# Rows scattered without the last layer norm, which the experts fold into their own norm, gate and epsilon

## The chip, the cores and the metric

The kernel runs on one core of one Trainium2 chip. The metric is device time in microseconds (us) of one execution, lower is better. The engines are PE (matrix products), DVE (VectorE), ACT (ScalarE), POOL (GpSimd) and SP (the engine that issues most transfers).

## The reference

Two transformer layers over 2 batches of 2048 tokens with 256 features:

```python
x = _layernorm(x + _L0_attn_ref(x, ...))     # causal attention with ALiBi, 16 heads
x = _layernorm(x + _L0_ffn_ref(x, ...))      # sparse product in frequency space
x = _layernorm(x + _L1_attn_ref(x, ...))     # channel attention, then its own norm, gamma and beta
x = _layernorm(x + _L1_ffn_ref(x, ...))      # routed experts
```

`_layernorm(x)` is `(x - mean) / sqrt(var + 1e-5)`. The last layer routes each token to one of 8 experts:

```python
aff = x @ centroids.T
eid = argmax(aff)
alpha = sigmoid(sum(x * centroids[eid]))
xn = (x - mean(x)) * rsqrt(var(x) + 1e-5)
xln = xn * ln_g[eid] + ln_b[eid]
ffn = relu(xln @ w1[eid] + b1[eid]) @ w2[eid] + b2[eid]
out = x + alpha * ffn
```

The x that enters the experts is the output of the third layer norm. Its mean is zero and its variance is var/(var + eps), so a norm of it can be worked out from the moments of the row before that norm.

## The kernel before

Tokens are handled in 8 tiles (g = 0 to 7) of 512 tokens, each of four 128-token blocks; batch 0 is tiles 0 to 3. The first layer's attention fills the first 920 us and is not touched.

**The back stage.** A planner (`BackPlan`) writes, once, a fixed order of steps for each engine: it takes again and again the step that could start first by its own cost estimates. The order in which PE uses turned tiles is a list written by hand, `TURNS`: O (output product of attention 0), S (spectral product), C (channel product of attention 1), A (affinities with the centroids). Each C tile goes: turn on PE (L1417), copies by ACT (L1782), product on PE (L1444, L1449), squares by ACT (L1811) and one root (L1814), `Scale` on DVE (L2067, L2073), `ShiftBeta` on POOL (L2470), `Combine` on DVE (L2081). The result is the row x before the third layer norm. Each A tile goes: turn (L1417), copies (L1782), `Affinity` (L1468), copy (L1788), turn back (L1476), then on DVE `Best` (L2194 to L2199, which expert), `Choose`, on PE `Count`, on DVE `PlaceRows` (the row's place among its expert's rows), and on POOL `Scatter` (L2484), which sends four blocks of rows to DRAM by indirect transfers.

For each of the 8 tiles the third layer norm is: `Moments` on DVE (4 of L2003, 4 of L2007), `Roots` on ACT (L1761), `Shift` on DVE (L2091, L2094) and `End` on ACT (4 of L1800), which normalises the rows in place. `Best` multiplies the largest affinity by this norm's inverse root (L2195) and stores it beside the row for the gate. `Scatter` waits for `End`.

After `PlaceRows(4)` the step `ChooseSoon` finds the experts of the first three slot tiles. SP then reads three row numbers and, once all products are done, fetches rows for slot tiles 0 to 2. `normalise_rows(0)` stands inside `PlaceRows(7)`, the last route.

**The expert stage.** 39 slot tiles of 128 rows. PE does for each `turn` (L1623), `hide` (L1635, product with w1) and `unhide` (L1647, product with w2). The steady loop of PE is hide(i+1), turn(i+2), unhide(i). That of DVE is turn_own(i+2), which reads the expert's number by `value_load` (L1612) and writes gain and shift (L2323), rectify(i+1) (L2343), normalise(i+3), finish(i), and in every third pass gates for three tiles. That of ACT is rectify, the two roots (L1761) and in every third pass three exponentials (L1871) for the gates. The rows' norm on DVE reads:

```python
take_moments(dve, m, s, n, [row])        # L2003, L2007
invert_roots(dve, m, s, n, 1)            # L2013, waits for ACT's root, L1761
dve.tensor_scalar(m.xn[i % 2], row, m.moments[:, n % NORMS, 0, 0:1], m.rstd[:, n % NORMS, 0:1], ALU.subtract, ALU.mult)
```

Of the kernel before, what the change touches and what calls it, by code (L numbers as in the profile page):

```python
# [14 lines left out]
P = 128  # L15
# [35 lines left out]
SOON = 3  # L51
# [3 lines left out]
NORMS = 4  # L55

# [489 lines left out]
Roots = namedtuple("Roots", "i eps")  # L546
Shift = namedtuple("Shift", "i stage g")
End = namedtuple("End", "i stage g turned")
# [26 lines left out]
Scatter = namedtuple("Scatter", "route normed")  # L575
# [6 lines left out]
def last_with(banks, route, bank):  # L582
# [7 lines left out]
    " C0 C1 C2 C3 A0 A1 C4 A2 C5 A3 C6 C7 A4 A5 A6 A7").split()]  # L590


class BackPlan:
# [7 lines left out]
    def __init__(self):  # L601
# [3 lines left out]
        self.todo = [(stage, g) for stage in "OSCFA" for g in range(TILES)]  # L605
# [164 lines left out]
    def norm_choices(self):  # L770
# [5 lines left out]
        for stage in "OSF":  # L776
            for g in range(TILES):
                if (stage, g) in self.norm_of:
                    continue
                ready = self.at(("second", g) if stage == "F" else ("add", stage, g))  # L780
                if ready is not None:
                    yield max(ready, last), 2, self.moments, (i, stage, g, max(ready, last))
                    break

    def moments(self, i, stage, g, ready):
# [3 lines left out]
        if stage == "F":  # L789
            self.todo.remove((stage, g))  # L790
# [7 lines left out]
    def root(self, i):  # L798
        self.n_rooted += 1
        self.run("act", Roots(i, 0), self.ROOTS, self.done["moments", i], ("roots", i))  # L800
# [12 lines left out]
    def end_choices(self):  # L813
        i = next((i for i in range(self.n_ended, self.n_shifted) if self.norms[i][0] != "O"), None)
        if i is not None:
            stage, g = self.norms[i]
            ready = self.at(("shift", i), *([("turn", self.turn_of.get(("A", g)))] if stage == "F" else []))
            if ready is not None:
                yield ready, 1, self.end, (i, ready)

    def end(self, i, ready):
# [3 lines left out]
        turned = 2 * self.turn_of["A", g] + 2 if stage == "F" else 0  # L825
        self.run("act", End(i, stage, g, turned), self.APPLY, ready, ("end", stage, g), ("end of", i))
# [88 lines left out]
    def route_choices(self, engine):  # L915
        for r, tiles in enumerate(ROUTES):
            for kind, on, step, cost, needs in (
                    ("hot", "dve", Best(r), 1300,
                     [("affinity turned", tiles[-1]), ("gram", tiles[-1] // TPB), ("shift of", "F", tiles[-1])]
# [6 lines left out]
                    ("scatter", "pool", Scatter(r, 0), 1270 * BPT * len(tiles),  # L926
                     [("place", r), ("end", "F", tiles[-1])] + [("scatter", r - 1)] * (r > 0))):
# [3 lines left out]
                if ready is not None:  # L931
                    if kind == "scatter":
                        step = step._replace(normed=self.end_of["F", tiles[-1]])
# [35 lines left out]
class Memory:  # L969


    def __init__(self, nc, ctx, t, out):
# [6 lines left out]
        def carve(at, shape, dt=F32, parts=P):  # L979
# [5 lines left out]
            if len(shape) > 1:  # L985
# [9 lines left out]
        self.eps_col = sb("eps_col", [P, 3])  # L995
# [24 lines left out]
        self.rstd_of = {stage: self.part_max[0][:, i * 2:i * 2 + 2, :, :].rearrange("p a h c -> p (a h c)")  # L1020
                        .rearrange("p (g r) -> p g r", g=TILES) for i, stage in enumerate("OF")}
        pairs = [half.rearrange("p (a r) -> p a r", a=2) for row in (self.neg_max, self.max_rest)
                 for half in (row[:, 0:2 * BPT], row[:, 2 * BPT:])]
        self.squares, self.std_c, self.rstd_c, self.top = pairs
# [125 lines left out]
class Signals:  # L1150


    def __init__(self, nc, ctx):
# [42 lines left out]
        self.rows_chosen = sem("rows_chosen")  # L1196
# [562 lines left out]
def root_moments(act, m, s, i, rows, eps):  # L1759
    act.wait_ge(s.moment, i + 1)  # L1760
    act.activation(m.std[:, i % NORMS, 0:rows], m.moments[:, i % NORMS, 0:rows, 1], ACTF.Sqrt,  # L1761
                   bias=m.eps_col[:, eps:eps + 1]).then_inc(s.rooted, 1)


def rstd_place(m, step):

    return m.rstd[:, step.i % NORMS, :] if step.stage == "S" else m.rstd_of[step.stage][:, step.g, :]


def scalar_back(nc, m, s, plan):  # L1770
    act = nc.scalar
    b0, b1 = FOLD_BANKS
    act.wait_ge(s.vector_set, 4)
    for step in plan.act:
# [15 lines left out]
        elif isinstance(step, Roots):  # L1790
            root_moments(act, m, s, step.i, BPT, step.eps)

        elif isinstance(step, End):
            j = step.i % NORMS
            act.wait_ge(s.norm_shift, plan.end_of[step.stage, step.g])
            if step.turned:
                act.wait_ge(s.turned, step.turned)
# [64 lines left out]
def scalar_experts(nc, m, s, plan):  # L1862
# [25 lines left out]
    root_moments(act, m, s, row_norm[0], 1, 0)  # L1888
    root_moments(act, m, s, row_norm[1], 1, 0)
    scalar_pads(nc, m, s)  # L1890
    gates(range(SOON))
    rectify_own(0)
# [944 lines left out]
```

## Time and profile before

| | |
|---|---|
| median of 3 runs | 1398.23 us (1397.38 to 1404.84) |
| the profiled execution's own time | 1393.97 us |
| span of the profile | 1392.2 us |
| PE busy over the span | 1329.6 us (96%) |
| DVE busy | 1069.0 us (77%) |
| ACT busy | 837.8 us (60%) |
| POOL busy | 263.8 us (19%) |

The span is from the first to the last instruction. The 1.8 us between span and the execution's own time are start and end. Busy shares are means over stages with different limits, so a stage has to be read by itself; the rows below do that for the channel and routing stage (1037 to 1097 us from the span's start) and for the experts (1098 us to the end).

### The profile page before, as it was taken

What the parts mean: (1) busy time and instruction counts of PE and PEld (TensorE: products, weight loads), DVE (VectorE), ACT (ScalarE), POOL (GpSimd) and SP (SyncE); (2) the same over time, 40 slices, a digit from 0 to 9 for tenths busy, and PEclk for the clock granted to TensorE, in tenths of its full rate; (3) what the DMA queues carried; (4) which work ended last, traced back from release to release, by engine and by line L of the source; (5) the groups of instructions that cost most, each with busy time, mean ns of one, the idle gap of its engine ahead of it and who ended that gap; (6) DMA issues with size and microseconds to landing.
All of it is one profiled execution on the core that took longest, in us unless ns stands there. A gap on an engine that the chain in (4) does not pass through costs nothing. (4 is left out here: it accounts for less than half of the span.)

```text
span 1392.2 us, 45529 instructions
## 1 busy us (share of the span) xinstructions
PE 1329.6 (96%) x19104; PEld 801.5 (58%) x19104; DVE 1069.0 (77%) x1991; ACT 837.8 (60%) x1767; POOL 263.8 (19%) x440
## 2 busy tenths in 40 slices
PE   8999999999999999999999999999987699999998
PEld 3544334434444444444444444587766589999997
DVE  2567989989899899899898992476567777766776
ACT  3446668778788688686886886533347333343342
POOL 4332012102111121121021111100126411111111
PEclk9999999999999999999999999999999899999999
DMA  7795401212112212112210000303616565445441
GB/s 228 219 213 133 80 17 37 46 32 50 41 40 46 44 31 48 42 40 48 69 49 4 3 3 2 119 31 117 239 32 212 194 226 181 167 176 186 169 176 71
DMA packets 78230, 134.44 MB, mean 97 GB/s; under 512 B 12370, under 2 KB 64843, under 8 KB 72652
## 3 DMA queue, kind: packets, MB, share of 16 engines
q1 hardware_dynamic: 60556, 109.63, 27.2%
q10 hardware_dynamic: 14064, 13.47, 3.1%
q0 software_dynamic: 3408, 8.43, 1.7%
q8 instruction: 152, 2.49, 0.8%
q14 instruction: 50, 0.41, 0.1%
HBM read 68.01 MB, written 23.11 MB: 65 GB/s over the span
## 5 line engine op out<-in xcount | busy, mean ns | idle before, releaser
L1964 DVE TENSOR_REDUCE part_max<-pair 128x2 f32<-128x1024 f32 (+2 forms) x576 | 641.8, 1158 | 63.0 <-PE pair L1329 32.0
L1748 ACT ACTIVATE big<-pair 128x512 f32<-128x512 f32 (+1 forms) x1120 | 580.2, 610 | 150.7 <-PE pair L1360 142.6
L1360 PE MATMUL pair<-big 128*32 128x512 bf16 (+3 forms) x5120 | 346.5, 349 | 6.7 <-DMA big<-max_t 2.8
L1329 PE MATMUL pair<-big 128*32 128x512 bf16 (+3 forms) x5120 | 340.9, 348 | 11.4 <-DVE part_max L1964 9.4
L1382 PE MATMUL pair<-big 128*17 128x512 f32 (+3 forms) x2560 | 288.2, 529 | 0.9 <-POOL big L2447 0.8
L1329 PEld LDWEIGHTS pair<-big 128*32 128x32 bf16 x5120 | 129.3, 96 | 185.6 <-DVE part_max L1964 94.2
L1360 PEld LDWEIGHTS pair<-big 128*32 128x32 bf16 x5120 | 126.8, 96 | 188.8 <-ACT big L1748 118.8
L1761 ACT ACTIVATE std<-moments,eps_col 128x1 f32<-128x1 f32 (+1 forms) x102 | 30.1, 295 | 235.0 <-DVE moments L2007 235.0
L1635 PE MATMUL pair<-big,tok 128*128 128x128 f32 x1248 | 148.0, 277 | 5.3 <-DVE big L2323 5.1
L1635 PEld LDWEIGHTS pair<-big,tok 128*128 128x128 f32 x1248 | 146.6, 194 | 9.4 <-DVE big L2323 7.7
L2447 POOL TENSOR_SCALAR_AFFINE_SELECT big<-big 128x512 f32<-128x512 f32 x128 | 80.0, 635 | 323.3 <-ACT big L1748 323.3
L1647 PE MATMUL pair<-big 128*128 x624 | 141.0, 379 | 0.0
L1647 PEld LDWEIGHTS pair<-big 128*128 128x128 f32 x624 | 115.6, 190 | 14.1
L1382 PEld LDWEIGHTS pair<-big 128*17 128x17 f32 x2560 | 68.5, 96 | 33.6 <-issue 4.5
L2492 POOL DMA_INDIRECT out<-big x39 | 38.4, 984 | 251.8 <-DVE big L2364 251.8
L1336 PE MATMUL pair<-masks,ident_b 128*32 128x64 bf16 x2048 | 86.1, 193 | 0.0
L1336 PEld LDWEIGHTS pair<-masks,ident_b 128*32 128x32 bf16 x2048 | 53.8, 97 | 28.9 <-issue 25.3
L1268 PE MATMUL pair<-big 128*32 128x512 f32 x512 | 60.0, 613 | 1.1 <-issue 0.8
L2323 DVE TENSOR_SCALAR big<-pair,cent_columns 128x128 f32<-128x128 f32 x78 | 28.4, 406 | 35.9 <-issue 27.7
L1880 ACT ACTIVATE big<-pair,cent_columns 128x128 f32<-128x128 f32 x156 | 44.3, 365 | 18.5 <-issue 11.0
L1933 DVE SCALAR_TENSOR_TENSOR big<-pair,big 128x512 f32<-128x512 f32 x32 | 22.1, 692 | 38.7 <-ACT big L1726 38.7
L2419 POOL TENSOR_TENSOR big<-big 128x512 bf16<-128x512 f32 x32 | 37.0, 1163 | 65.9 <-ACT big L1731 65.9
(213 smaller groups left out, 1209.2 us busy)
## 6 DMA issues: line engine op xcount, KB each, us to landing
tok<-big SPq DMA_DIRECT2D x39, 1024.0 KB, 4.7
big<-in_L_ffn_w SPq DMA_DIRECT2D x16, 1024.0 KB, 14.3
big<-split_dram SPq DMA_DIRECT2D x216, 64.0 KB, 2.9
split_dram<-big ACTq DMA_DIRECT2D x32, 384.0 KB, 4.4
big<-split_dram SPq DMA_DIRECT2D x42, 256.0 KB, 4.3
big<-routed_dram SPq DMA_DIRECT2D x39, 129.0 KB, 2.1
big<-in_c_query_rows SPq DMA_DIRECT2D x8, 512.0 KB, 4.8
big<-in_L_attn_x SPq DMA_DIRECT2D x8, 512.0 KB, 4.5
```

The source lines that it names most:

```text
L1268: mm = pe.matmul(m.bank[b][q:q + STRIPE, :], m.w_qkv0[side][:, c, o:o + STRIPE], m.x_t[step.tile % 2][:, c, :], start=(c == 0), stop=(c == ...
L1329: mm = pe.matmul(bank[q:q + STRIPE, o:o + w], m.q_op[slot][:, step.qt, h, step.r * P + q:step.r * P + q + STRIPE], m.k_op[slot][:, h, step ...
L1336: mm = pe.matmul(bank[q:q + STRIPE, o + w - P + half:o + w - P // 2 + half], m.ident_b[:, q:q + STRIPE], m.masks[:, 1, half:half + P // 2] ...
L1360: mm = pe.matmul(m.bank[step.bank][k:k + STRIPE, n * w:(n + 1) * w], m.k_op[slot][:, h, step.kb * P + k:step.kb * P + k + STRIPE], m.q_op[ ...
L1382: mm = pe.matmul(m.sums[32 * h:32 * h + HD + 1, q0:TILE], m.v_aug[:, b * BPB + kb, g * GH + h, :], m.p_ring[:, place, h, at:at + TILE - q0 ...
L1635: mm = pe.matmul(m.bank[b][:, j * P:(j + 1) * P], w1[:, c, f * P:(f + 1) * P], m.xln_t[i % 2][:, c, :], start=(c == 0), stop=(c == KC - 1))
L1647: mm = pe.matmul(m.bank[b][:, 0:D], m.hidden_t[i % 2][:, f, :], m.w2[:, bass.ds(e, 1), f, :].rearrange("p a n -> p (a n)"), start=(f == 0) ...
L1748: act.activation(m.p_ring[:, step.place, step.heads[0]:step.heads[-1] + 1, step.at:step.at + w], m.bank[step.bank][:, 0:len(step.heads) * ...
L1880: done = act.activation(m.hidden_t[i % 2][:, j, :], m.bank[b][:, j * P:(j + 1) * P], ACTF.Relu, bias=col[:, j, bass.ds(e, 1)])
L1964: dve.tensor_reduce(m.part_max[(step.u * QT + step.qt) % 2][:, step.r, step.heads[0]:step.heads[0] + n, step.c], banks[:, :, 0:w], X, ALU. ...
L2447: pool.affine_select(weights, weights, pattern=[[0, GH], [1, P]], compare_op=ALU.is_ge, fill=zero, base=0, channel_multiplier=-1).then_inc ...
L2492: pool.indirect_dma_start(m.out_rows, bass.IndirectOffsetOnAxis(ap=m.xs[i % ROWS_AHEAD][:, D + 1:D + 2].bitcast(I32), axis=0), m.final[i % ...
```

## The change

The third layer norm is no longer applied in the back stage. The steps `Moments`, `Roots`, `Shift` and `End` of stage F are gone for all 8 tiles. `Scatter` waits for `Combine` in place of `End`. The centroids are stored with the sign turned, so that `Best` takes the least value and writes it straight beside the row (one operation, L2195, goes). The rows that reach the experts are the rows before the norm. For each slot tile DVE works out `row_eps`, ACT takes two roots in place of one (the second for both norms together), DVE inverts the two at once, the gate's exponential takes its scale and bias from columns in place of immediates, the gate is scaled by the first inverse root, and the root of the result takes its epsilon from `row_eps`. The first three gates are made later in the order (on DVE behind `choose_rows`, on ACT behind the first rectify and the third root). In `TURNS` the tile A4 moves ahead of C6 and A5 ahead of C7.

```diff
 TURNS = ...
     "O0 O1 O2 S0 O3 S1 S2 S3 O4 O5 O6 S4 O7 S5 S6 S7"
-    " C0 C1 C2 C3 A0 A1 C4 A2 C5 A3 C6 C7 A4 A5 A6 A7").split()]
+    " C0 C1 C2 C3 A0 A1 C4 A2 C5 A3 A4 C6 A5 C7 A6 A7").split()]
...
-        for stage in "OSF":
+        for stage in "OS":
...
-                    ("scatter", "pool", Scatter(r, 0), 1270 * BPT * len(tiles),
-                     [("place", r), ("end", "F", tiles[-1])] + [("scatter", r - 1)] * (r > 0))):
+                    ("scatter", "pool", Scatter(r), 1270 * BPT * len(tiles),
+                     [("place", r)] + [("scatter", r - 1)] * (r > 0))):
...
+def root_row(act, m, s, i, n):
+
+    k, var = i % ROWS_AHEAD, m.moments[:, n % NORMS, 0, 1:2]
+    act.wait_ge(s.moment, n + 1)
+    act.activation(m.row_std[:, k, 0:1], var, ACTF.Sqrt, bias=m.eps_col[:, 0:1])
+    act.activation(m.row_std[:, k, 1:2], var, ACTF.Sqrt, bias=m.eps_col[:, 2:3], scale=1.0 + EPS).then_inc(s.rooted, 1)
+
+
+def root_result(act, m, s, i, n):
+    act.wait_ge(s.moment, n + 1)
+    act.activation(m.std[:, n % NORMS, 0:1], m.moments[:, n % NORMS, 0, 1:2], ACTF.Sqrt,
+                   bias=m.row_eps[:, i % ROWS_AHEAD, :]).then_inc(s.rooted, 1)
...
-            act.wait_ge(s.rows_in[k], 16 * (i // ROWS_AHEAD + 1))
-            act.activation(m.gate[:, k:k + 1], m.xs[k][:, D:D + 1], ACTF.Exp, scale=-1.0).then_inc(s.gate_exp, 1)
+            act.wait_ge(s.xn_set, i + 1)
+            act.activation(m.gate[:, k:k + 1], m.xs[k][:, D:D + 1], ACTF.Exp, bias=m.eps_col[:, 3:4],
+                           scale=m.row_rstd[:, k, 0:1]).then_inc(s.gate_exp, 1)
...
         elif isinstance(step, Moments):
-            if step.stage == "F":
-                dve.wait_ge(s.combined, step.g + 1)
             take_moments(dve, m, s, step.i, m.norm_rows(step.stage, step.g))
...
-            top = m.top[:, i % 2, :]
+            least = m.tok[:, blocks, D]
...
-            step_done(dve.tensor_reduce(top, affinity, X, ALU.max))
-            dve.tensor_tensor(m.tok[:, blocks, D], top, m.rstd_of["F"][:, tiles[0], :], ALU.mult).then_inc(s.rows_chosen, 1)
-            step_done(dve.tensor_tensor(equal, affinity, wide(top, shape, 2), ALU.is_equal))
+            step_done(dve.tensor_reduce(least, affinity, X, ALU.min))
+            step_done(dve.tensor_tensor(equal, affinity, wide(least, shape, 2), ALU.is_equal))
...
 def normalise_rows(dve, m, s, i, n):
-    row = m.xs[i % ROWS_AHEAD][:, 0:D]
-    dve.wait_ge(s.rows_in[i % ROWS_AHEAD], 16 * (i // ROWS_AHEAD + 1))
+
+    k = i % ROWS_AHEAD
+    row, mean, var = m.xs[k][:, 0:D], m.moments[:, n % NORMS, 0, 0:1], m.moments[:, n % NORMS, 0, 1:2]
+    dve.wait_ge(s.rows_in[k], 16 * (i // ROWS_AHEAD + 1))
     take_moments(dve, m, s, n, [row])
-    invert_roots(dve, m, s, n, 1)
+    dve.wait_ge(s.moment, n + 1)
+    dve.tensor_scalar(m.row_eps[:, k, :], var, EPS, EPS / 4, ALU.add, ALU.mult)
+    dve.wait_ge(s.rooted, n + 1)
+    dve.reciprocal(m.row_rstd[:, k, :], m.row_std[:, k, :]).then_inc(s.norm_inverse, 1)
+    dve.wait_ge(s.norm_inverse, n + 1)
     if i >= 2:
         dve.wait_ge(s.tile_turned, i - 1)
-    dve.tensor_scalar(m.xn[i % 2], row, m.moments[:, n % NORMS, 0, 0:1], m.rstd[:, n % NORMS, 0:1], ALU.subtract,
-                      ALU.mult).then_inc(s.xn_set, 1)
+    dve.tensor_scalar(m.xn[i % 2], row, mean, m.row_rstd[:, k, 1:2], ALU.subtract, ALU.mult).then_inc(s.xn_set, 1)
...
             dve.wait_ge(s.gate_exp, i + 1)
-            dve.tensor_scalar(g, g, 1.0, 2.0, ALU.add, ALU.mult).then_inc(s.gate_sum, 1)
+            dve.tensor_scalar(g, g, 2.0, m.row_rstd[:, k, 0:1], ALU.add, ALU.mult).then_inc(s.gate_sum, 1)
...
-    gates(range(SOON))
     rectify(0)
     normalise(2)
     turn_own(2)
     rectify(1)
     choose_rows(dve, m, s, step_done)
+    gates(range(SOON))
     finish(0)
...
-            pool.wait_ge(s.rows_chosen, step.route + 1)
-            pool.wait_ge(s.normed, step.normed)
+            pool.wait_ge(s.combined, tiles[-1] + 1)
```

## Rows read from the trace of the kernel before

**Rows 1.** Busy time by stretch: stretch, length, each engine (instructions), clock, DMA.

```profile
1150.00:1200.00 50.00, 50.00 (x348) 47.21 (x347) 34.68 (x124) 20.33 (x56) 6.88 (x7) 1.00 0.49 179
```

**Rows 2.** Timeline of one pass of the expert loop: start, length, engine, idle before.

```profile
1206.14 0.73 DVE L2323 TENSOR_SCALAR big<-pair,cent_columns 128x128 f32<-128x128 f32 x2 [0.73 <-issue]
...
1208.28 0.18 DVE L2007 BATCH_NORM_AGGREGATE moments<-stats 128x2 f32<-128x6 f32 x1
1208.49 0.29 ACT L1761 ACTIVATE std<-moments,eps_col 128x1 f32<-128x1 f32 x1 [1.57 <-DVE moments L2007]
1208.82 0.16 DVE L2013 RECIPROCAL rstd<-std 128x1 f32<-128x1 f32 x1 [0.36 <-ACT std L1761]
...
1213.13 0.73 DVE L2323 TENSOR_SCALAR big<-pair,cent_columns 128x128 f32<-128x128 f32 x2 [1.13 <-issue]
```

**Rows 3.** Waits from 1155 to 1376 us: total, times, longest.

```profile
DVE big L2323 <- issue: 25.4, 29, 1.3
...
DVE recip_l L2331 <- ACT recip_l L1871: 8.3, 10, 0.9
...
DVE big L2323 <- PE pair L1623: 1.6, 2, 1.1
```

**Rows 4.** Line L1612, the load of an expert's number: shortest/median/longest ns.

```profile
L1612 DVEq TENSOR_LOAD <-tile_expert x39: 302/562/998, 1091.2 to 1374.1; - x39
```

**Rows 5.** Groups by line and shape from 1100 us: count, busy us, mean ns.

```profile
L2323 DVE TENSOR_SCALAR big<-pair,cent_columns 128x128 f32<-128x128 f32 x76 | 27.7, 407 | 35.9 <-issue 27.7 <-PE pair L1623 8.2
...
L1761 ACT ACTIVATE std<-moments,eps_col 128x1 f32<-128x1 f32 x76 | 22.4, 295 | 164.5 <-DVE moments L2007 164.5
```

**Rows 6.** The same view, further down: the gates' exponentials.

```profile
L1871 ACT ACTIVATE recip_l<-big 128x1 f32<-128x1 f32 x39 | 5.0, 192 | 0.1
```

**Rows 7.** Groups by line and shape from 1000 to 1095 us.

```profile
L2484 POOL DMA_INDIRECT routed_dram<-tok,position x28 | 28.2, 1008 | 17.6 <-DVE position L2228 10.4 <-issue 7.2
...
L1800 ACT ACTIVATE tok<-tok,shift,part_max 128x256 f32<-128x256 f32 x32 | 16.6, 596 | 0.5 <-DVE shift L2094 0.5
...
L1811 ACT ACTIVATE big<-pair 128x256 f32<-128x256 f32 x28 | 10.4, 377 | 8.6 <-PE pair L1449 8.6
```

**Rows 8.** Timeline: a root on ACT and the instruction right behind it.

```profile
1066.15 0.30 ACT L1814 ACTIVATE neg_max<-neg_max,eps_col 128x4 f32<-128x4 f32 x1
...
1066.35 1.06 ACT L1782 ACTIVATE big<-pair 128x512 f32<-128x512 f32 x2
```

**Rows 9.** Timeline of channel tiles 5 to 7 and the affinity tiles behind.

```profile
1048.55 2.07 ACT L1800 ACTIVATE tok<-tok,shift,part_max 128x256 f32<-128x256 f32 x4
...
1050.68 1.07 ACT L1782 ACTIVATE big<-pair 128x512 f32<-128x512 f32 x2
...
1051.80 0.39 PE L1444 MATMUL pair<-acc_t,part_max 128*128 128x512 bf16 x1 [0.64 <-ACT big L1782]
...
1059.24 1.23 DVE L2081 TENSOR_TENSOR tok<-tok,big 128x1024 f32<-128x1024 f32 x1
...
1061.18 0.39 PE L1444 MATMUL pair<-acc_t,part_max 128*128 128x512 bf16 x1 [0.64 <-ACT big L1782]
...
1067.97 0.38 PE L1444 MATMUL pair<-acc_t,part_max 128*128 128x512 bf16 x1
...
1075.58 1.09 PE L1417 MATMUL pair<-ident,tok 128*128 128x128 f32 x8
...
1078.67 1.09 PE L1417 MATMUL pair<-ident,tok 128*128 128x128 f32 x8
```

**Rows 10.** Timeline of the last route and the first expert tile.

```profile
1082.22 0.14 PEld L1476 LDWEIGHTS pair<-ident,masks 128*128 128x128 f32 x1 [0.66 <-ACT masks L1788]
...
1088.43 0.19 DVE L2194 TENSOR_REDUCE max_rest<-pair 128x4 f32<-128x32 f32 x1
...
1092.30 0.43 DVE L2003 BATCH_NORM_STATS2 stats<-big 128x6 f32<-128x256 f32 x1 [1.14 <-DMA big<-routed_dram]
...
1097.85 5.53 PE L1635 MATMUL pair<-big,tok 128*128 128x128 f32 x32 [1.90 <-DVE big L2323]
```

More of the change, by code:

```diff
@@ L545 @@
 Moments = namedtuple("Moments", "i stage g")
-Roots = namedtuple("Roots", "i eps")
+Roots = namedtuple("Roots", "i")
 Shift = namedtuple("Shift", "i stage g")
-End = namedtuple("End", "i stage g turned")
+End = namedtuple("End", "i stage g")
 ShiftBeta = namedtuple("ShiftBeta", "g m")
@@ L574 @@
 PlaceRows = namedtuple("PlaceRows", "route")
-Scatter = namedtuple("Scatter", "route normed")
+Scatter = namedtuple("Scatter", "route")
 Busy = namedtuple("Busy", "count")
@@ L604, in __init__ @@
         self.done = {"loaded": 9000}
-        self.todo = [(stage, g) for stage in "OSCFA" for g in range(TILES)]
+        self.todo = [(stage, g) for stage in "OSCA" for g in range(TILES)]
         self.turns, self.turns_used, self.uses = [], 0, 0
@@ L779, in norm_choices @@
                     continue
-                ready = self.at(("second", g) if stage == "F" else ("add", stage, g))
+                ready = self.at(("add", stage, g))
                 if ready is not None:
@@ L799, in root @@
         self.n_rooted += 1
-        self.run("act", Roots(i, 0), self.ROOTS, self.done["moments", i], ("roots", i))
+        self.run("act", Roots(i), self.ROOTS, self.done["moments", i], ("roots", i))
     def shift_choices(self):
@@ L816, in end_choices @@
             stage, g = self.norms[i]
-            ready = self.at(("shift", i), *([("turn", self.turn_of.get(("A", g)))] if stage == "F" else []))
-            if ready is not None:
-                yield ready, 1, self.end, (i, ready)
+            ready = self.done["shift", i]
+            yield ready, 1, self.end, (i, ready)
     def end(self, i, ready):
@@ L824, in end @@
         self.end_of[stage, g] = len(self.end_of) + 1
-        turned = 2 * self.turn_of["A", g] + 2 if stage == "F" else 0
-        self.run("act", End(i, stage, g, turned), self.APPLY, ready, ("end", stage, g), ("end of", i))
+        self.run("act", End(i, stage, g), self.APPLY, ready, ("end", stage, g), ("end of", i))
     def squares_choices(self):
@@ L918, in route_choices @@
                     ("hot", "dve", Best(r), 1300,
-                     [("affinity turned", tiles[-1]), ("gram", tiles[-1] // TPB), ("shift of", "F", tiles[-1])]
+                     [("affinity turned", tiles[-1]), ("gram", tiles[-1] // TPB)]
                      + [("hot", r - 1)] * (r > 0)
@@ L931, in route_choices @@
                 if ready is not None:
-                    if kind == "scatter":
-                        step = step._replace(normed=self.end_of["F", tiles[-1]])
                     yield ready, 0, self.run, (engine, step, cost, ready, (kind, r))
@@ L1790, in scalar_back @@
         elif isinstance(step, Roots):
-            root_moments(act, m, s, step.i, BPT, step.eps)
+            root_moments(act, m, s, step.i)
         elif isinstance(step, End):
```

69 lines of the change are left out of this document (34 added, 35 removed).

## The prediction

> **What bounds the kernel now.** I read the busy time by stretch first, and it misleads: from 1150 to 1200 us PE is busy for all 50.00 us and DVE for 34.68 [rows 1]. That looks like a PE bound with 30% of DVE to spare. The view of waits says otherwise. Between 1155 and 1376 us DVE's first step of a pass waited for PE twice, for 1.6 us in all, while its idle time is "issue", 25.4 us in 29 passes, and the gates' wait for ACT, 8.3 us in 10 [rows 3]. So DVE walks its loop without ever being held by PE for long: its idle time lies inside its own chain. One pass took 6.99 us from L2323 to L2323 [rows 2]. In it the chain is moments, ACT's root, inverse: 0.36 us of DVE idle while ACT works 0.29 us [rows 2]. The "issue" time is the load of the expert's number ahead of L2323, 0.30 to 1.00 us with a median of 0.56 [rows 4]. The reader is to see that PE and DVE run level, and that whatever lengthens DVE's serial chain lengthens the kernel, though DVE's share is 70%.
>
> The other stretch that counts is serial as well. From the channel product of C4 to the first hide, each C tile with an A tile takes 9.38 us (product of C5 at 1051.80, of C6 at 1061.18), the C tile without one 6.79 (C7 at 1067.97), an A tile alone 3.09 (turns at 1075.58 and 1078.67) [rows 9]. The last route was turned back at 1082.22, but its `Best` began at 1088.43, behind `ChooseSoon`, the last `Moments` and two routes on DVE; the first rows' norm began at 1092.30 and hide(0) at 1097.85 [rows 10].
>
> **The change, part by part. Removed from the back stage.** 32 of L1800 (16.6 us of ACT) [rows 7], 32 statistics on DVE, 8 roots, 8 `Shift`. Most of it lay beside PE's work. What sat on the path is ACT's order: `End` ran from 1048.55 to 1050.62, so the copy of the affinity and the copies of C5 at 1050.68 stood behind it and the product waited 0.64 us for them [rows 9]. Without `End` the copies could begin when the first half of the turn is there; I take 0.7 us for each of C5 and C6 and 0.8 for C4, bounds 0.3 and 1.2 each. C7 gains nothing new (next term). Sum: 2.2 us earlier. Of the fold of batch 1 I expect nothing: its waits are for PE and DVE steps that stay.
>
> **Moved: A4 ahead of C6, A5 ahead of C7.** A4 adds an A tile, 3.09 less the 0.4 that `End` cost there, 2.7. C6 to C7 grows from 6.79 to 9.38 less 0.7, 8.7: 1.9. One more `Count` on PE: 0.4. So C7's product starts 2.7 + 1.9 + 0.4 - 2.2 = 2.8 us later, at 1070.8. In return only A6 and A7 lie behind it. From the start of a C product to the end of its `Combine` is 1059.24 + 1.23 - 1051.80 = 8.7 us [rows 9]; from the turn of A7 to its turn back 1082.22 + 0.33 - 1078.67 = 3.9, without `End` 3.5 [rows 9, 10]. So `Best(7)` could start at 1070.8 + 8.7 + 3.5 + 0.3 for hand-overs = 1083.3 in place of 1088.43, since `ChooseSoon` (its route 4 is done before C6) and routes 4 to 6 are behind DVE by then. From `Best(7)` to the first rows' norm was 1092.30 - 1088.43 = 3.87 us [rows 10], with one `PlaceRows` in it that can now come earlier; I take 3.3, so that norm begins at 1086.6. Head start: 5.7 us, bounds 2 and 10. SP's fetch of the first rows hangs on `ChooseSoon` and C7's product, both past by 1075: hidden, with 10 us to spare. The gates moved on DVE lie ahead of finish(0), whose product is there already; about 0.3 us of them shows at tile 4, whose hide waits for DVE.
>
> **Added to every slot tile.** (a) The second root. A root of one column with a pointer for its bias is 295 ns [rows 5]. A root began at 1066.15 and lasted 0.30, the next instruction began at 1066.35 [rows 8]: a pitch of 0.20. DVE waits for the second, so its idle 0.36 becomes 0.56: 0.20 us. Lower bound 0.10 (the two overlap more), upper 0.30 (not at all). (b) `row_eps` on DVE lies inside that wait: nothing; it needs about one hand-over (0.04) and one small operation, well under 0.36 us; with no cover, 0.2. (c) An inverse of two columns for one: nothing. (d) The exponentials get two pointers for two numbers. Without pointers one takes 192 ns [rows 6]. ACT with two pointers on 256 columns is 596 ns, without 377 [rows 7]: 0.22 for two; one pointer is 295 against 192. The gates' sum on DVE waits 0.83 us on average for the first [rows 3], so 0.20 more, and the following two come slower, 0.05: 0.25 us for each group of three, bounds 0 and 0.5. The gates' sum itself has a pointer for a number: at most the same 0.1, in the upper bound. No engine waits behind ACT for this otherwise.
>
> 34 norms of rows lie in the loop behind hide(4) (slot tiles 5 to 38) and 12 groups of gates: 34 x 0.20 + 12 x 0.25 = 6.8 + 3.0 = 9.8 us, bounds 3.4 (0.10 and 0) and 16. Ahead of it the norms of rows 0 and 1 delay hide(0) by 0.4 us and the one of row 4 delays hide(4) by 0.2; with the gates' 0.3 that is 0.9.
>
> The Trainium skill, ScalarE: Activation LUTs, section What ACT_TABLE_LOAD costs, says that each pointer operand adds about 93 ns to an ACTIVATE and that back-to-back ones overlap by about 93 ns. The traced 295 against 192 ns agrees [rows 5, 6]. An estimate by that page: the second root costs 280 - 93 = 187 ns, the first exponential 186 ns more, and the ones behind it come at 279 ns; the sum would be 6.4 + 3.4. No row shows an exponential with pointers.
>
> **Sum.** -5.7 + 0.9 + 9.8 = +5.0 us on the profiled execution's 1393.97, of which 1392.2 are span: 1399.0. The median of the runs shown is 4.3 us above that execution, so the median comes to 1403.
>
> **Rivals.** (1) Not slower: ACT overlaps the pair of roots (0.10) and the exponentials cost nothing. Then 3.4 + 0.9 - 5.7 = -1.4, and with a head start of 10 us, -5.7: a median of 1392 to 1397. For it: a row with two exponentials back to back would be shorter than their sum. Against it: the pitch of 0.20 behind a root [rows 8]. It decides if DVE's chain grows by less than 0.13 us a tile. (2) POOL becomes the wait. A scatter is 4 x 1.26 = 5.0 us of POOL (1008 ns and 0.26 idle each) [rows 7] and cannot be broken off. If POOL takes up scatter 4 or 5 just ahead of `ShiftBeta(7)`, `Combine(7)` comes up to 4.7 us late and A7, the last route, with it. For it: scatters now wait for less and crowd ahead of C7. Against it: `ShiftBeta` has about 1.3 us to spare, and before one scatter lay there too. Then +9.7, a median of 1408. (3) DVE has room after all: PE sets the pace and the additions vanish, as the shares of rows 1 suggest. Then about -5, 1393. Against it: two waits for PE in 30 passes [rows 3]. (4) The load of the expert's number, 0.30 to 1.00 us for no reason that I can name [rows 4], falls otherwise with the new phases: 0.1 us on its mean is 3.4 us either way. This is part of the range.
>
> **Chances.** Forecast 0.52, rival 1 0.20, rival 2 0.18, rival 3 0.10. The forecast's own range is -1 to +9 us, by the bounds of 0.20 and of the head start; with a tenth left out on each side over all cases it is -5 to +13: 1393 to 1411. A measurement tells about 0.5%, 7 us. Faster than that takes rival 1 or 3 with the largest head start: 0.08. Slower takes rival 2 or the upper third of the forecast: 0.30. Within 0.5%: 0.62.
>
> **What would show each step.** In the profile after: idle of DVE ahead of the inverse of the rows' norm 0.56 us (0.46 in rival 1); the gates' wait near 1.1 us; mean pass of DVE 0.28 us longer and PE with gaps ahead of hide in most passes, so that PE's busy share in the experts falls; hide(0) near 1092.5 (1097 in rival 2, with `Combine(7)` waiting for POOL); C7's product near 1070.8. The prediction is wrong if PE stays without gaps, if the head start is over 10 us because the planner orders the fold otherwise, or if PE waits on a `Count`.

## The result, and the profile after

The changed kernel takes 1405.3 us against 1397.0, medians of 15 runs each; the ratio is 1.006, with a 95% interval of 1.0046 to 1.0074. It is 0.6% slower: 8.3 us, where +5.0 us on the profiled execution and a median of 1403 were forecast. The profiled execution has a span of 1403.2 us against 1392.2.

The busy time of the same stretch as in [rows 1], in the changed kernel:

```profile
1150.00:1200.00 50.00, 49.52 (x339) 46.27 (x339) 35.57 (x127) 19.88 (x58) 6.88 (x7) 1.00 0.48 175
```

PE has lost half a microsecond of the 50 and DVE has gained 0.9. The waits of DVE from 1155 to 1376 us (total, times, longest), to be held against [rows 3]:

```profile
DVE big L2334 <- issue: 22.5, 29, 1.1
DVE recip_l L2343 <- ACT recip_l L1879: 10.9, 10, 1.1
DVE rstd L2022 <- ACT std L1771: 10.5, 29, 0.4
DVE part_max L2278 <- ACT part_max L1766: 10.4, 29, 0.4
```

The gates' wait is 1.09 us in place of 0.83, and the two waits for PE have gone. One norm of the rows, in the timeline of the changed kernel (start, length, engine, idle before); [rows 2] has the old one:

```profile
1207.50 0.42 DVE L2012 BATCH_NORM_STATS2 stats<-big 128x6 f32<-128x256 f32 x1
1207.95 0.18 DVE L2016 BATCH_NORM_AGGREGATE moments<-stats 128x2 f32<-128x6 f32 x1
1208.16 0.15 DVE L2276 TENSOR_SCALAR part_max<-moments 128x1 f32<-128x1 f32 x1
1208.16 0.29 ACT L1765 ACTIVATE part_max<-moments,eps_col 128x1 f32<-128x1 f32 x1 [1.27 <-DVE moments L2016]
1208.37 0.28 ACT L1766 ACTIVATE part_max<-moments,eps_col 128x1 f32<-128x1 f32 x1
1208.68 0.17 DVE L2278 RECIPROCAL part_max<-part_max 128x2 f32<-128x2 f32 x1 [0.36 <-ACT part_max L1766]
```

The second root begins 0.21 us behind the first. From the end of the moments to the inverse it is 1208.68 - 1208.13 = 0.55 us; before it was 1208.82 - 1208.46 = 0.36 [rows 2]. The idle time is still written as 0.36, because the new small operation L2276 (`row_eps`) fills the rest: whoever reads only the idle column sees no change.

Now the view that the prediction did not use: PE's own timeline, by the starts of its first operation in each pass (L1631, the hide product).

```profile
1198.61 3.73 PE L1631 MATMUL pair<-big,tok 128*128 128x128 f32 x32
1202.18 0.38 PE L1619 MATMUL pair<-ident,big 128*128 128x128 f32 x2
1202.39 3.62 PE L1643 MATMUL pair<-big 128*128 x16
1206.60 3.84 PE L1631 MATMUL pair<-big,tok 128*128 128x128 f32 x32 [0.59 <-DVE big L2334]
...
1213.95 3.73 PE L1631 MATMUL pair<-big,tok 128*128 128x128 f32 x32
```

From start to start it is 7.99 us with the idle 0.59 at its end, and 7.35 for the next. From the eleventh tile on PE's passes in the changed kernel go 7.9, 7.35, 7.24, 8.0, 7.35, 7.24, 8.4, 7.35, 7.24 and so on: one in three is long, the one behind the gates, and the other two are at or near 7.24. PE has a gap ahead of hide in 9 passes of the 30 from 1155 to 1376 us, not in most of them as the prediction's sign said:

```profile
PE pair L1631 <- DVE big L2334: 5.6, 9, 0.9
```

In the kernel before, 25 of the 34 passes behind hide(4) are 7.24 or 7.25 us to the hundredth, as if the engine ran free. It nearly did. The rest of this document divides each profile at PE's first product of tile 0, 4 and 38, called hide(0), hide(4), hide(38); these are worked out from the starts in the timelines. The times are us, and the number load is the mean over the loads behind hide(4):

```
kernel                       hide(0)  to hide(4)  to hide(38)  per pass  DVE's number load  span
before                       1097.85     30.48      248.02      7.295        0.61           1392.2
changed                      1100.63     31.91      254.65      7.490        0.49           1403.2
changed, profiled again      1102.59     31.74      255.38      7.511        0.50           1405.7
old turns                    1105.99     32.99      255.98      7.529        0.49           1410.9
new turns alone, on before   1100.69     30.78      246.88      7.261        0.58           1394.2
one root                     1101.65     31.37      250.37      7.364        0.55           1399.2
numbers in the gates         1099.91     31.71      251.70      7.403        0.52           1399.2
gates late                   1101.34     31.73      251.73      7.404        0.68           1400.6
gates late, on before        1098.60     30.88      246.43      7.248        0.80           1391.8
gates late, one root         1098.59     32.05      248.75      7.316        0.69           1395.2
gates late, early load       1101.92     32.57      248.06      7.296        0.48           1398.4
  the same, on before        1102.50     31.02      246.43      7.248        0.57           1395.8
  the same, one root         1103.50     32.57      248.06      7.296        0.51           1400.0
  the same, and old turns    1098.56     31.56      246.43      7.248        0.51           1392.4
```

The ledger of the changed kernel against the one before, profile against profile: hide(0) 2.8 us later, 1.4 more up to hide(4), 6.6 more in the loop, 0.1 behind it; 11.0 in all. Each row is one execution, and hide(0) is counted from the start of the span. The first channel product C0, which lies ahead of everything that the change touches there, already starts anywhere from 990.4 to 996.7 us in these 14 profiles (991.25 before, 991.44 changed, 994.72 in its second profile, 996.68 with the old turns). So differences of hide(0) between rows are not differences of the kernels; the head start is read further down from C3's product, which follows C0's by 27.7 us in every profile.

### The profile page after: what moved, and what is told of

It is laid out like the page before. It is cut to its first block and busy times, and to the rows that moved or that the text cites. A ratio compares the mean times of both kernels' runs of the same rounds, so it can differ in the third digit from the quotient of the medians.

```text
span 1403.2 us, 45417 instructions
## 1 busy us (share of the span) xinstructions
PE 1329.7 (95%) x19078; PEld 798.4 (57%) x19078; DVE 1062.0 (76%) x1943; ACT 836.4 (60%) x1766; POOL 265.2 (19%) x440
## 5 line engine op out<-in xcount | busy, mean ns | idle before, releaser
L1631 PE MATMUL pair<-big,tok 128*128 128x128 f32 x1248 | 148.9, 278 | 15.9 <-DVE big L2334 15.9
L1631 PEld LDWEIGHTS pair<-big,tok 128*128 128x128 f32 x1248 | 146.3, 194 | 22.2 <-DVE big L2334 20.9
L1771 ACT ACTIVATE std<-moments,part_max 128x1 f32<-128x1 f32 x39 | 11.5, 295 | 95.6 <-DVE moments L2016 95.6
L2334 DVE TENSOR_SCALAR big<-pair,cent_columns 128x128 f32<-128x128 f32 x78 | 28.4, 406 | 37.5 <-issue 25.6
L1765 ACT ACTIVATE part_max<-moments,eps_col 128x1 f32<-128x1 f32 x39 | 11.5, 294 | 72.0 <-DVE moments L2016 64.5
```

Of the source, the lines that this page charges most:

```text
L1631: mm = pe.matmul(m.bank[b][:, j * P:(j + 1) * P], w1[:, c, f * P:(f + 1) * P], m.xln_t[i % 2][:, c, :], start=(c == 0), stop=(c == KC - 1))
```

## The experiments

Ratios are to the kernel before, with 95% intervals.

**The order of turns alone, both ways.** The changed kernel with the old order, and the kernel before with the new one:

```
-    " C0 C1 C2 C3 A0 A1 C4 A2 C5 A3 A4 C6 A5 C7 A6 A7").split()]
+    " C0 C1 C2 C3 A0 A1 C4 A2 C5 A3 C6 C7 A4 A5 A6 A7").split()]
```

> The changed kernel with the old order of turns (C6 and C7 ahead of A4 and A5); the norm stays folded. Theory, that moving A4 and A5 forward is close to neutral (it makes C7 later, and saves routes 4 to 6 ahead of the last): C7's product near 1067, Best(7) between 1086 and 1089, hide(0) within 2 us of the changed kernel's 1100.6, and 1.004 to 1.008 of the kernel before. Rival, that the move is what ate the head start: hide(0) at 1095 or earlier, and 1.002 or less. Rival 2, that the 4.5-us stall ahead of hide(0) in the profile belongs to the new order: it is gone here.

> The kernel before with the new order of turns alone; its last norm stays. Theory: the loop is that of before (mean pass 7.28 us), hide(0) moves by -1 to +3 us, and the ratio to before is 0.999 to 1.003. Rival, that the new order itself costs the 0.6%: 1.004 or more, with hide(0) 5 us or more later.

Measured: 1.0065 (1.0051 to 1.008) and 0.9997 (0.9986 to 1.0007). The move of A4 and A5 is worth nothing in either direction; the 0.6% belongs to the fold. Of the details, `Best(7)` at 1090.0 was outside the expected 1086 to 1089, and hide(0) at 1106.0 was later than expected. But this execution was 5.2 us late at C3's product already; counted from there hide(0) comes at 81.6 us, and at 81.5 in the changed kernel. A stall ahead of hide(0), which rival 2 gave to the new order, is here too: from the first rows' norm to DVE's first L2334 it is 8.2 us, 9.8 in the changed kernel and 4.8 before. So it does not belong to the new order.

**One root.** It leaves out the exact second epsilon: rows and gate share 1/sqrt(var + eps).

```
-    act.activation(m.row_std[:, k, 0:1], var, ACTF.Sqrt, bias=m.eps_col[:, 0:1])
-    act.activation(m.row_std[:, k, 1:2], var, ACTF.Sqrt, bias=m.eps_col[:, 2:3], scale=1.0 + EPS).then_inc(s.rooted, 1)
+    act.activation(m.row_std[:, k, 0:1], var, ACTF.Sqrt, bias=m.eps_col[:, 0:1]).then_inc(s.rooted, 1)
```

> The changed kernel with one root per row norm in place of two (it leaves out the exact second epsilon; rows and gate use the same 1/sqrt(var + eps)). Theory, that DVE's chain is the bound and waits for the second root: 0.20 us less in each of 37 norms, 7.4 us in all, 1.001 of before, mean pass 7.29. Rival, that the lengthening of the pass has another cause (the small DVE operations, or where the expert's number load falls): 2 us or less, 1.004 to 1.006 of before.

**Numbers for pointers in the gates.** It leaves out the fold of the norm into the gate.

```
-            act.activation(m.gate[:, k:k + 1], m.xs[k][:, D:D + 1], ACTF.Exp, bias=m.eps_col[:, 3:4],
-                           scale=m.row_rstd[:, k, 0:1]).then_inc(s.gate_exp, 1)
+            act.activation(m.gate[:, k:k + 1], m.xs[k][:, D:D + 1], ACTF.Exp, scale=1.0).then_inc(s.gate_exp, 1)
...
-            dve.tensor_scalar(g, g, 2.0, m.row_rstd[:, k, 0:1], ALU.add, ALU.mult).then_inc(s.gate_sum, 1)
+            dve.tensor_scalar(g, g, 1.0, 2.0, ALU.add, ALU.mult).then_inc(s.gate_sum, 1)
```

> The changed kernel with numbers in place of pointers in the gates' exponential (bias and scale) and in the gates' sum; it leaves out the fold of the norm into the gate. Theory: the exponentials cost 377 ns against 192 and the sum 0.06 us more, 0.37 us a group; 12 groups and the first one give 4.5 to 5 us back, 1.003 of before, and a gate pass is 0.37 us shorter. Rival, that the gates cost no more than I had predicted (0.25) or nothing: 1.004 to 1.006 of before.

Measured: 1.0019 (1.0008 to 1.0029) with one root, 1.0039 (1.0026 to 1.0052) with numbers. The root gives 4.3 us of the loop back (254.65 to 250.37), where 0.20 in each of 37 norms was expected; the numbers give 3.0, where 4.5 to 5 was. The waits of DVE, first with one root, then with numbers:

```profile
DVE part_max L2277 <- ACT part_max L1765: 5.0, 29, 0.2
```

```profile
DVE recip_l L2342 <- ACT recip_l L1879: 9.0, 10, 0.9
```

The wait for the root falls from 10.4 to 5.0 us in 29 norms, 0.19 each, and the one for the exponentials from 1.09 to 0.90. So both terms of the prediction are where it put them. But both repay less than their 34 x 0.19 = 6.5 and 12 x 0.37 = 4.4, and in both the number load of DVE grew, from 0.49 to 0.55 and 0.52 us, which is 2 and 1 us over 34 passes. One exponential takes 377 ns with its two pointers (L1879, mean of 39) and 192 without.

**The changed kernel once more.**

> The changed kernel as it is, profiled once more, to see what of its profile recurs. Theory: the loop is the same to 0.02 us a pass (7.49) with PE's own pass 7.24 to 7.25; the 4.5-us stall of DVE's first L2334 ahead of hide(0) and the late affinity copies at 1062 and 1087 belong to one execution, and hide(0) lies within 3 us of 1100.6. Rival: they recur at the same places to 0.2 us, and are part of the change.

It took 1407.4 us. The loop recurs (7.511 us a pass) and the stall of 4.5 us ahead of hide(0) does not. The late affinity copies do, against the expectation: the one at 1062.50 starts 1.7 us behind the end of its product in the first profile, and the same one 1.7 us behind in the second (1065.57); the last one is 1.4 and 0.9 us late. It gave a second trace of the back stage, used below.

**Gates late.** DVE's sum and inverse of the gates leave the end of one pass for the place just ahead of `finish` in the next; ACT's exponentials stay. Made on the changed kernel, on the one before, and with one root:

```
             normalise(i + 3)
+        if (i - SOON) % 3 == 0:
+            gates([j for j in range(i, i + 3) if j < SLOT_TILES])
         finish(i)
-        if (i - SOON) % 3 == 2:
-            gates([j for j in range(i + 1, i + 4) if j < SLOT_TILES])
```

> The changed kernel with DVE's part of the gates (sum and inverse) moved from the end of one pass to just ahead of finish in the next; ACT's part stays where it is. Theory, that PE's own pass of 7.245 us is the floor and DVE's chain is over it only for want of 0.25 us a pass: the wait of 1.09 us for the exponentials (12 times, 0.38 us a pass) vanishes, DVE falls under PE, the loop gives 8 us back and no more: passes of PE 7.24 to 7.25 throughout, 1.000 of before. Rival 1, that DVE alone bounds: 13 us back, 0.997. Rival 2, that the wait for ACT only moves: 1.004 or more.

> The kernel before with the same move of DVE's part of the gates. Theory, that its loop is already within 1.1 us of PE's own pass (34 x 7.245 = 246.3 of 247.4 us): 0.999 of before, the gates' wait of 0.83 us gone without a return. Rival, the prediction's reading that DVE's chain bounds the loop and PE only runs level: 12 x 0.83 = 10 us back, 0.993.

> The changed kernel with the late gates and with one root per row norm (it leaves out the exact second epsilon). Theory: PE's pass is the floor, so this is the same as with late gates alone, 0.999 to 1.001 of before, and the two savings do not add. Rival, that they add: a further 6 us, 0.993 to 0.996.

Measured: 1.0041 (1.0027 to 1.0056), 0.9988 (0.9977 to 1.0) and 0.9991 (0.998 to 1.0003). The second came as expected, and its rival of 0.993 lies outside the interval. It decides what bounds the kernel before. PE's timeline in it, and DVE's waits:

```profile
1202.02 3.73 PE L1635 MATMUL pair<-big,tok 128*128 128x128 f32 x32
...
1209.27 3.73 PE L1635 MATMUL pair<-big,tok 128*128 128x128 f32 x32
...
1216.51 3.73 PE L1635 MATMUL pair<-big,tok 128*128 128x128 f32 x32
```

```profile
DVE big L2323 <- PE pair L1623: 32.9, 30, 1.4
DVE rstd L2013 <- ACT std L1761: 21.7, 60, 0.4
...
DVE big L2323 <- issue: 1.1, 1, 1.1
```

Ten microseconds of waiting were taken out of DVE's chain and the loop gained 1.6: PE repeats at 7.25 and 7.24 us, and DVE now waits for it in every one of the 30 passes. So 34 x 7.248 = 246.4 us is PE's floor, and the kernel before stood 1.6 us above it. The prediction's rival 3 was right about that kernel.

On the changed kernel the same edit did less than expected. The gates' wait is gone, but DVE still doesn't fall under PE:

```profile
DVE big L2334 <- issue: 25.2, 29, 1.2
DVE part_max L2278 <- ACT part_max L1766: 16.4, 30, 1.5
...
DVE big L2334 <- PE pair L1619: 1.1, 1, 1.1
```

Part of the wait moved: DVE reaches its next moments while ACT is still behind the exponentials, and waits 16.4 us for roots in place of 10.4. The number load took another part: 0.68 us on average in place of 0.49. Rival 2 of that run was right for these, and my 1.000 was wrong.

The third run met its number and not its theory, that the two savings do not add. They do: the loop falls from 251.73 to 248.75 us, because late gates alone had not brought the changed kernel down to PE's pass.

**The number load moved.** It goes to where DVE waits for ACT anyway. Made with late gates on the changed kernel, on the one before, with one root, and with one root and the old order of turns:

```
         take_moments(dve, m, s, n, [mixed])
+        if SOON <= i and i + 3 < SLOT_TILES:
+            experts[i + 3] = chosen_expert(dve, m, s, i + 3)
         invert_root(dve, m, s, n)
```

> The changed kernel (both roots, exact fold) with the late gates and, besides, DVE's load of the expert's number taken from ahead of L2334 to the place between the moments of the result and the inverse that waits for ACT's root. Theory, that late gates alone left the loop at 7.36 us a pass because the number load grew to 0.69 us (it is slow where the transfer of the next w1 fills the DMA engines) and because roots come later behind ACT's table loads: the load now lies beside a wait of 0.36 us, the pass comes to PE's own 7.245 to 7.27, 3 us less than with late gates alone, 1.001 to 1.002 of before. Rival, that the load only moves its time: the idle ahead of the inverse grows by as much, pass 7.36, 1.004.

> The kernel before with late gates and the early number load. Theory: its loop with late gates alone stood at PE's own 7.24 to 7.25 us in every pass, so nothing more comes of it: 0.998 to 0.999 of before. Rival, that DVE's chain still counts somewhere: 0.996 or less.

> The changed kernel with one root per row norm, late gates and the early number load (it leaves out the exact second epsilon). Theory: the loop is at PE's floor (7.245), so what is left against the kernel before is the back stage alone; that has given no head start, so 0.998 to 0.999, the same as the kernel before with late gates. Rival, the prediction's reading that the fold gives 5.7 us ahead of hide(0) once the loop takes nothing back: 0.994 to 0.995.

> The same kernel (one root, late gates, early number load; it leaves out the exact second epsilon) with the old order of turns. Theory: with the old order ChooseSoon ends late, and SP's first fetch of rows hangs on it, so Best(7) comes 2 us earlier than in the kernel before but the first rows' norm does not; 0.998 to 1.000, within 0.1% of the same kernel with the new order. Rival, that the new order is what loses the head start: 0.995.

Measured: 1.0014 (1.0002 to 1.0025), 0.9999 (0.9988 to 1.001), 1.0001 (0.9987 to 1.0014) and 1.0011 (0.9999 to 1.0023). The first is inside its expected 1.001 to 1.002. The second and third lie 0.1% above what was expected, with the expected values in their intervals; the third excludes its rival of 0.994 to 0.995. The fourth, expected at 0.998 to 1.000 and within 0.1% of the third, is 0.1% above it.

In the first, with both roots and all the pointers, every pass of PE but one is 7.24 or 7.25 us, and from hide(5) on PE's product never waits for DVE. The pass behind hide(4) is 8.98 us, because the hide product in it takes 5.47 us in place of 3.84. The clock granted to PE was 0.50 there (the lower of its two levels, 1.2 for 2.4 GHz), after PE had waited 2.4 us for DVE. The last but two figure is the clock:

```profile
1134.70:1138.10 3.40, 3.40 (x18) 3.40 (x18) 2.02 (x8) 2.01 (x4) 0.31 (x1) 0.50 0.77 277
```

Without these 1.6 us its loop would be 246.4 us, PE's floor. The same drop behind hide(4) is in three other profiles with the fold (old turns; gates late, one root; early load, one root) and in none of the four without it; in the other six with the fold the clock stays at 1.00. DVE's waits in the first run:

```profile
DVE rstd L2022 <- ACT std L1771: 18.4, 29, 1.1
DVE big L2334 <- PE pair L1619: 14.9, 19, 1.1
DVE part_max L2278 <- ACT part_max L1766: 14.9, 31, 0.8
```

The fold's cost in the loop behind hide(5) can therefore be hidden. What comes out with the exact fold is still 0.14% slower than the kernel before, 2 us, and its interval just leaves out 1; with one root it is the kernel before, to about 0.1%. No version here beats it by more than its interval.

## Why the prediction came out as it did

**What bounds the kernel: wrong for the kernel before, right for the changed one.** I set aside PE's 50.00 busy microseconds of 50 [rows 1], because DVE hardly ever waited for PE [rows 3]. The step that failed is "So DVE walks its loop without ever being held by PE for long: its idle time lies inside its own chain". The one pass that it measured, 6.99 us [rows 2], was itself shorter than PE's 7.245, so DVE could run faster than PE. DVE had slack, and its number load ate it unseen. Take the 242 such loads between 1130 and 1390 us in seven profiles (before, changed twice, one root, numbers, gates late on both kernels) by the DMA engines' busy share in the load's first 0.3 us. The 72 with a share under 0.3 took 0.304 us on average and at most 0.315; the 137 with 0.9 or more took 0.805, between 0.30 and 1.00. Over all ten profiles with the load in its old place it is 101 loads at 0.307 (one took 0.51) and 198 at 0.795. Two stretches of the changed kernel, each one load, the last but one figure being the DMA engines' busy share:

```profile
1211.46:1211.76 0.30, 0.30 (x3) 0.28 (x2) 0.30 (x1) 0.10 (x1) 0.00 (x0) 1.00 0.29 82
1217.99:1218.94 0.95, 0.95 (x6) 0.85 (x5) 0.40 (x1) 0.35 (x2) 0.00 (x0) 1.00 0.95 354
```

What fills the DMA engines is the transfer of the next w1 (1024 KB, 30 of them from 1150 to 1376 us), which SP issues when PE has hidden a tile. My reading is that a DVE that runs ahead of PE meets that transfer more often, and that one that is late finds it over. The mean load fits this roughly: 0.80 us where DVE waits for PE in every pass, 0.61 before, 0.49 in the changed kernel, but 0.58 with the new turns alone, whose pass is shorter than before. That the transfer lengthens the load is a coincidence in the records, not shown as a cause; no run here took the transfer away. Without the load, DVE's pass was 7.277 - 0.608 = 6.67 us before; with a load of 0.30 it is 6.97, 0.27 below PE's 7.245. In the changed kernel it is 7.490 - 0.487 = 7.00, and 7.31 with the shortest load: over PE. The change used up a slack that the prediction said was not there. That DVE sets the pace of the changed kernel is shown by the runs that shorten its chain and get the loop back, down to PE's 246.4.

**The added roots: right.** 0.20 us a norm was forecast, 0.19 measured, by the pair of starts, by the interval to the inverse, and by taking it away. The Trainium skill, ScalarE: Activation LUTs, section What ACT_TABLE_LOAD costs, has the figures from which the prediction estimated 187 ns; the traces agree.

**The gates: right in place, too small.** 0.25 us a group was forecast. The exponentials made the wait 0.19 longer as worked out (1.09 for 0.90 with numbers). I kept the gates' sum only in the upper bound: with a pointer it takes 0.20 us in place of 0.14, three times a group. That makes 0.37.

**The sum of the loop.** By these terms 34 x 0.19 + 12 x 0.37 = 10.9 us; the passes without their loads grew by 0.335 x 34 = 11.4. The shorter loads gave back 0.12 x 34 = 4.1, and DVE's loop grew by 7.3 where 9.8 was forecast (6.6 between PE's products). The prediction had this as rival 4, "falls otherwise with the new phases: 0.1 us on its mean is 3.4 us". The size was right and the cause was nameable.

**The head start: wrong.** hide(0) was to come 5.7 us earlier, with bounds of 2 and 10, less 0.4 for two norms. It did not come earlier. In us from the start of C3's product (1018.98 before, 1019.17 changed), worked out from the timelines:

```
                      before  forecast  changed  again  gates late, on before
product of C4          23.45     -       21.77   21.80     21.77
product of C5          32.83     -       31.38   31.15     31.38
product of C7          49.00   51.8      54.51   55.41     47.77
Best(7)                69.46   64.3      68.34   71.68     68.22
first rows' norm       73.32   67.6      70.90   74.17     74.59
hide(0)                78.87   73.5      81.46   80.15     80.34
```

Three steps failed.

First, the 2.2 us for `End`. C4's product did begin 1.5 us earlier from the start of the span, at 1040.94, but that is no work of the change: with `End` still in place, "gates late, on before" has the same 21.77 and 31.38 us. The profile before was the odd one. The product L1570 between C3 and C4 took 5.38 us in it, at a granted clock of 0.59, and 3.69 in the other:

```profile
1029.00:1033.00 4.00, 3.38 (x8) 2.73 (x9) 2.16 (x10) 0.63 (x3) 0.00 (x0) 0.59 0.00 0
```

For C5 the step that failed is "the copies of C5 at 1050.68 stood behind it". They stood behind PE's turn as well, which began 1.39 us ahead of them. Without `End` the copies still begin 1.37 us behind the turn. First before, then changed:

```profile
1049.29 1.09 PE L1417 MATMUL pair<-ident,tok 128*128 128x128 f32 x8
```

```profile
1047.80 1.09 PE L1413 MATMUL pair<-ident,tok 128*128 128x128 f32 x8
...
1049.17 1.32 ACT L1792 ACTIVATE big<-pair 128x512 f32<-128x512 f32 x2 [0.95 <-PE pair L1413]
```

So `End` cost PE's path nothing, and I had counted a gain three times that did not exist once.

Second, C7's product was forecast for 1070.8 and began at 1073.68: C5 to C6 took 13.85 us, not 11.8, and C6 to C7 9.28, not 8.7. Of the 2.0 more between C5 and C6, the late affinity copy at 1062.50 has up to 1.7. In the second profile C6 to C7 is 10.39 us, because C6's two products took 2.97 and 2.33 us in place of 1.89 each, at a granted clock of 0.51 (1068.3 to 1071.7).

Third, "`ChooseSoon` ... and routes 4 to 6 are behind DVE by then". They are, because they moved ahead of C6's `Scale`. From C7's product to `Best(7)` 12.5 us was forecast; it took 13.8 in the first profile, of which the late last copy is 1.4, and 16.3 in the second. The eight profiles with fold and new order have 13.8 and 14.0 in two and 15.9 to 16.5 in six. In the second profile of the changed kernel:

```profile
1073.54 2.60 POOL L2482 TENSOR_TENSOR tok<-tok,big 128x256 f32<-128x256 f32 x4
...
1073.82 2.34 DVE L2231 TENSOR_TENSOR spectral<-acc_t,small 1x8 f32<-1x8 f32 x1 [0.20 <-issue]
...
1074.12 0.30 ACT L1822 ACTIVATE neg_max<-neg_max,eps_col 128x4 f32<-128x4 f32 x1
...
1076.84 0.28 DVE L2240 TENSOR_TENSOR spectral<-spectral,small 1x128 f32<-1x128 f32 x1
...
1079.34 0.15 DVE L2254 TENSOR_TENSOR tile_row<-spectral,small 1x3 int32<-1x3 f32 x1
1079.42 0.16 DVE L2076 RECIPROCAL max_rest<-neg_max 128x4 f32<-128x4 f32 x1
1079.61 1.66 DVE L2082 SCALAR_TENSOR_TENSOR big<-pair,max_rest,big 128x256 f32<-128x256 f32 x4
```

The root of C6 is done at 1074.42 and its inverse begins at 1079.42: five microseconds in which DVE works off route 4, with L2231 held up until 1076.16 (see the last section), and the chain of `ChooseSoon` (L2240 to L2254). In the first profile it is 4.2 us. Behind it come `Combine(6)`, then C7's. The end of the last route in the first profile of the changed kernel:

```profile
1081.59 1.23 DVE L2090 TENSOR_TENSOR tok<-tok,big 128x1024 f32<-128x1024 f32 x1
...
1084.70 0.64 PE L1464 MATMUL pair<-big,cent_columns 128*32 128x128 f32 x16 [0.51 <-ACT big L1792]
...
1086.72 0.28 ACT L1798 ACTIVATE masks<-pair 128x128 f32<-128x128 f32 x1 [2.07 <-PE pair L1464]
...
1087.51 0.19 DVE L2201 TENSOR_REDUCE tok<-pair 128x4 f32<-128x32 f32 x1 [2.37 <-PE pair L1472]
...
1090.08 0.43 DVE L2012 BATCH_NORM_STATS2 stats<-big 128x6 f32<-128x256 f32 x1 [1.03 <-issue]
```

`Best(7)` starts at 1087.51 where 1083.3 was forecast (in the second profile at 1094.12), and the copy L1798 starts 1.4 us after the product that it copies has ended, for no reason that the rows show (ends of products are modelled in the profile). With the old order and the fold `Best(7)` comes 65.6 us behind C3's product, but the first rows' norm only 1097.05 - 1090.01 = 7.0 us later. The stage of the kernel before has 6.4 and 6.6 there in two profiles and 3.9 in the one of [rows 10]. My reading is that the fetch of the first rows, which hangs on `ChooseSoon`, holds the norm there; no run moved that fetch by itself. Either order loses what the other gains, which fits that the two turn experiments show nothing. From `Best(7)` to the norm I had 3.3 us and it was 2.6 (2.5 in the second profile); that step was right. So the norm did come 2.2 us earlier in the first profile, where 5.7 was forecast, and the stall behind it took that away.

What is left of the head start is nothing, to about 1 us. From C3's product to hide(0) the eight profiles with fold and new order take 79.7 to 82.7 us, mean 80.8, the two with fold and old order 81.6 and 79.9, the three of the kernel before's stage 78.9, 80.3 and 80.6, the new turns alone 80.2. The times say the same: the changed kernel's 8.3 us are its loop and the stretch to hide(4), about 8; and the one with gates late and early load loses 2.1 us behind hide(0) against the kernel before and is 2 us slower.

**Up to hide(4)** 0.5 us was forecast (0.2 for the norm, 0.3 for the gates) and 1.4 came, 1.3 in the second profile. Of it 0.8 lies between hide(3) and hide(4) (6.46 us for 5.64) and stays with one root (6.48). That is where the prediction put the moved gates with 0.3; no run moved them back.

**The rivals.** (1) fell: the pair of roots overlaps to 0.20, not 0.10. (2) did not decide: in the first profile `ShiftBeta(7)` starts at 1078.87, right behind a scatter, but ends 0.07 us ahead of the last `Scale` that `Combine(7)` needs as well. (3) was right about the kernel before and wrong about the changed one; I gave it 0.10, and it deserved a look at PE's period. So +5.0 came near +8.3 by luck in part, through two errors of opposite sign: the loop was put 2.5 us too high, the head start 5.7 too high the other way.

## What to carry to other kernels

Before calling an engine free, take the start-to-start interval of the other one over many passes: an interval that repeats to 0.01 us in pass after pass points to a bound that the list of waits does not show, and taking waits out of the other engine tests it. Slack can hide in an instruction that stretches with traffic, so a chain may look full and still have room, here 0.27 us of 7.25; an addition is hidden up to there and shows beyond. When tiles are reordered to bring the last one forward, list what the in-order engine between them now does first, not only what is no longer behind. And a few microseconds between two single profiles are no gain yet: take them from the last event that the change does not touch, and look at the granted clock in between.

## What the runs showed of the hardware

Loading a number from memory into a register of DVE's sequencer takes 0.30 us with quiet DMA engines and 0.80 on average with busy ones, as above.

An operation on DVE of 0.15 us (L2231, 1 x 8) took 2.34 us in the second profile, beginning inside `ShiftBeta` on POOL (1073.54 to 1076.14) and ending with it (1076.16); POOL's four operations followed one another and DVE did not get in between. In the first profile the same line, ahead of `ShiftBeta`:

```profile
1069.07 0.15 DVE L2231 TENSOR_TENSOR spectral<-acc_t,small 1x8 f32<-1x8 f32 x1 [0.20 <-DVE acc_t L2226]
```

It took 2.34 to 2.41 us in four of the eight profiles with fold and new order and at most 0.39 in the other ten. In these four C6 to C7 is 10.38 to 10.45 us in place of 9.24 to 9.34; the granted clock was 0.5 for 3.4 us from 1065.8, 1067.2, 1068.2 and 1068.3 us on, ahead of the operation, and in the other ten there is no such drop between 1060 and 1075 us. That the slower PE is what moved the operation into `ShiftBeta` is a reading. The Trainium skill, SBUF — State Buffer, section SBUF: two separate sides, says that VectorE with two inputs from SBUF and a GpSimd operation that reads SBUF exclude each other for a whole instruction; the trace agrees, and shows the loser kept out over four of them.

A stall across engines, ahead of hide(0) in the first profile:

```profile
1093.90 6.41 SPq L2716 DMA_DIRECT2D routed_dram<-big  x3
...
1095.42 5.51 ACTq L1858 DMA_DIRECT2D routed_dram<-big  x4
...
1099.85 0.73 DVE L2334 TENSOR_SCALAR big<-pair,cent_columns 128x128 f32<-128x128 f32 x2 [4.51 <-remote]
```

In this stretch the sequencers of SP and ACT take steps of 0.68 to 0.71 us for register operations that otherwise take 0.02 to 0.19, and DVE starts 4.5 us late. Steps of 0.68 to 0.72 us stand between 1077 and 1106 us in 9 of the 14 profiles (in one of them a single step), with the fold and without, and the same kernel has them in one execution and not in the next. DVE's long wait is rarer. From the first rows' norm to its first L2334 it is 9.8, 8.3 and 8.2 us in three profiles (changed; gates late, one root; old turns) and 4.8 to 5.4 in the other eleven. These three have the fold and the earliest first norms of all, 70.9, 71.4 and 72.6 us behind C3's product. So it is not shown that the change has no part in it; the cause is open.
